# Attention and expert kernel: key and query parts stored in DRAM as 128-row blocks, read back in eight transfers a batch, with the query reads ahead of a row of maxima

## The reference

```python
q = proj(x1t, Wq, bq)                       # x1 = layernorm(x), 512 positions, 8 heads x 16
k = proj(x2t, Wk, bk)                       # x2 = ctx
v = proj(x2t, Wv, bv)
scores = jnp.einsum('bhqd,bhkd->bhqk', q, k) / jnp.sqrt(D_HEAD)
attn = jax.nn.softmax(scores, axis=-1)
out = jnp.einsum('bhqk,bhkd->bhqd', attn, v)
...
x = x + jnp.tanh(g_xattn[0]) * out
h = _rmsnorm(_layernorm(x), rms_weight)     # 4096 rows of 512
w_dense = top-2 of softmax(h @ router_w), normalised
moe = sum over e of w_dense[e] * (silu(h @ w_gate[e]) * (h @ w_up[e])) @ w_down[e]
sh = silu(h @ sw_gate) * (h @ sw_up) @ sw_down
x = x + jnp.tanh(g_ffn[0]) * (moe + sh)
```

## Time and profile before

| | |
|---|---|
| time, median of 3 runs | 1412.91 us (1408.93 to 1428.1) |
| the profiled execution, its own time | 1411.02 us |
| its span in the trace | 1409.1 us |
| PE, DVE, ACT, POOL busy | 92%, 69%, 62%, 61% of the span |
| attention, up to the last turning of maxima | 880 us |
| mean share of time in which the 16 DMA engines are busy | 72% from 376 to 867 us |

### The profile page before, as it was taken

The page is one execution under the profiler, slowest core; times in us unless marked ns, Lnnn a source line. Parts: engine busy times, 40 slices in busy tenths (PEclk is TensorE's granted clock), DMA queues, the critical chain, the costliest instruction groups (busy, mean ns, idle before and its releaser), DMA issues.

```text
span 1409.1 us, 34589 instructions
## 1 busy us (share of the span) xinstructions
PE 1290.6 (92%) x12274; PEld 680.4 (48%) x12274; DVE 974.3 (69%) x1661; ACT 874.1 (62%) x1720; POOL 863.3 (61%) x1267
## 2 busy tenths in 40 slices
PE   2899899999998899889999988799999999999997
PEld 0233333333333333323333332387788878888885
DVE  4988889999987798888889887556654323333332
ACT  2488788888877788778878876534334333333332
POOL 8547677767787687867787752640214555555553
PEclk7799999999999999999999999999999999999999
DMA  6567777777777677677777664376654888886565
GB/s 177 166 175 212 205 215 210 206 211 193 194 207 191 187 194 197 189 187 208 192 196 193 196 164 112 122 209 145 126 176 90 203 197 202 198 190 112 111 108 80
DMA packets 161348, 248.28 MB, mean 176 GB/s; under 512 B 33733, under 2 KB 58956, under 8 KB 161182
## 3 DMA queue, kind: packets, MB, share of 16 engines
q1 hardware_dynamic: 142926, 208.70, 53.5%
q0 software_dynamic: 18256, 37.38, 14.5%
HBM read 141.06 MB, written 103.88 MB: 174 GB/s over the span
## 4 chain that ended last, share of the span: by engine, by line
PE 42%; DMA 13%; SPq 12%; issue 12%; POOL 9%; DVE 9%; ACT 2%; POOLq 1%; DVEq 0%; another core or an unknown queue 0%; ACTq 0%
PE m_banks L969 19%; SPq L471 7%; PE bank L926 6%; PE bank L895 6%; DVE row_max L1142 6%; PE m_banks L873 4%; DMA arena<-pv_d 4%; DMA arena<-parts_q 4%; DMA parts_k<-arena 3%; PE bank L901 2%; POOL xs L793 2%; SPq L532 2%; PE bank L857 1%; PE bank L851 1%; PE bank L991 1%
## 5 line engine op out<-in xcount | busy, mean ns | idle before, releaser
L1142 DVE TENSOR_REDUCE row_max<-m_banks 128x2 f32<-128x1024 f32 x512 | 614.8, 1221 | 98.5 <-PE m_banks L873 89.7
L1426 ACT ACTIVATE arena<-bank 128x512 f32<-128x512 f32 x1024 | 554.4, 605 | 97.7 <-PE bank L895 89.9
L895 PE MATMUL bank<-arena 112*32 112x512 bf16 x4096 | 338.2, 384 | 11.9 <-ACT arena L1426 7.2
L926 PE MATMUL bank<-arena 128*32 128x512 f32 x2048 | 283.2, 603 | 1.9 <-issue 1.6
L895 PEld LDWEIGHTS bank<-arena 112*32 112x32 bf16 x4096 | 113.1, 95 | 275.5 <-ACT arena L1426 136.3
L873 PE MATMUL m_banks<-arena 48*128 48x512 bf16 x1024 | 176.6, 391 | 58.2 <-DMA arena<-parts_q 29.2
L805 POOL DMA_INDIRECT out<-xs,ids x71 | 112.3, 1581 | 172.9 <-ACT xs L1508 140.7
L969 PE MATMUL m_banks<-w_ring,h_hi 128*128 x568 | 183.0, 403 | 0.0
L1497 ACT ACTIVATE arena<-m_banks 128x256 f32<-128x256 f32 x103 | 39.5, 384 | 189.7 <-PE m_banks L969 179.3
L873 PEld LDWEIGHTS m_banks<-arena 48*128 48x128 bf16 x1024 | 40.3, 94 | 194.7 <-issue 83.2
L694 POOL TENSOR_TENSOR arena<-arena 128x512 f32<-128x512 f32 x32 | 40.9, 1279 | 122.8 <-DMA arena<-pv_d 119.4
(11 more groups left out here) (182 smaller groups left out, 1997.9 us busy)
## 6 DMA issues: line engine op xcount, KB each, us to landing
pv_d<-arena SPq DMA_DIRECT2D x32, 512.0 KB, 4.4
w_ring<-split_d SPq DMA_DIRECT2D x60, 256.0 KB
parts_k<-arena SPq DMA_DIRECT2D x96, 128.0 KB
parts_q<-arena SPq DMA_DIRECT2D x96, 128.0 KB
arena<-parts_k SPq DMA_DIRECT2D x64, 192.0 KB
arena<-parts_q SPq DMA_DIRECT2D x64, 192.0 KB
arena<-in_w SPq DMA_DIRECT2D x36, 256.0 KB, 7.2
arena<-in_ctx SPq DMA_DIRECT2D x32, 256.0 KB, 3.7
```

The source lines that it names most:

```text
L895: last = nc.tensor.matmul(out[c, :], k_stack[b % 3][0:SHIFTED, h, kt * P + c.start:kt * P + c.stop], q_stack[b % 3][0:SHIFTED, h, :], star ...
L926: last = nc.tensor.matmul(pv_ps[2 * DH * j:2 * DH * (j + 1), :], v_ones[b % 3][:, kt, GROUP * g + j, :], probs[pair % 3][:, j, :], start=( ...
L1142: nc.vector.reduce_max(pair, m_ps[(STEPS * b + u) // 2 % M_PAIRS], AX_X).then_inc(s_mx, 1)
L1426: nc.scalar.activation(probs[group % 3][:, j, :], bank_of["scores", b, s], ACT.Exp, scale=float(DH) ** -0.5).then_inc(s_exp, 1)
```

## The change

`parts_d` gets four parts in place of three: for keys low, middle, high, high, for queries high, high, middle, low, so that each of the two stacked orders is three parts that lie side by side. The rows of the key and query weights and biases are permuted on the host (`rows_first`), so that a projected row is (channel, head), as it is in DRAM. A batch's parts are then written by two transfers each for keys and queries: the high part twice in one transfer, the middle and low part in another, which waits for both. The middle and low part lie side by side in SBUF (`held`). The reads are 4 and 4 transfers where they were 6 and 6. In SP's list the middle and low part of the query goes ahead of the key reads, and the query reads go ahead of the reciprocals and of the row of maxima, which also change places. The two stores of an expert's row become one.

```diff
-STORED = ((LO, MID, HI), (HI, MID, LO))
-FIRST = ((MID, HI, HI), (HI, HI, MID))
-SECOND = ((LO, MID, HI), (HI, MID, LO))
...
+STORED = ((LO, MID, HI, HI), (HI, HI, MID, LO))
+HELD = ((HI, LO, MID), (HI, MID, LO))
+FIRST_AT, SECOND_AT = (1, 0), (0, 1)
+READS = 8
+WRITES = 2
...
-                    sp.wait_ge(s_part, 4 * b + 2 * n + part)
-                sp.dma_start(parts_d[n][b % 2][STORED[n].index(part)].rearrange("d h l -> h d l"), parts[n][part]
+                    sp.wait_ge(s_part, 4 * b + 2 * n + 2)
+                rows = parts_d[n][b % 2].rearrange("t d h l -> (d h) t l")
+                at = STORED[n].index(part if part == HI else HELD[n][1])
+                sp.dma_start(rows[:, at:at + 2, :],
+                             parts[n][HI].unsqueeze(1).broadcast_to([P, 2, L]) if part == HI else held[n][:, 1:3, :]
                              ).then_inc(s_wr[n], DMA)
...
-                    for row, parts_at in ((LANE * a, FIRST), (LANE * (1 - a), SECOND)):
-                        for at, part, k in stored_runs(parts_at, n):
-                            sp.dma_start(lane(stack[row + at * DH:row + (at + k) * DH, :, :], a),
-                                         lane(src[part:part + k].rearrange("t d h l -> (t d) h l"), a)
-                                         ).then_inc(s_rd[b % 3], DMA)
+                    for row, at in ((LANE * a, FIRST_AT[n]), (LANE * (1 - a), SECOND_AT[n])):
+                        sp.dma_start(lane(stack[row:row + STACK, :, :], a),
+                                     lane(src[at:at + 3].rearrange("t d h l -> (t d) h l"), a)
+                                     ).then_inc(s_rd[b % 3], DMA)
...
                 if is_b(i + 2):
-                    if i + 2 > 0:
-                        read(i + 2, 0)
                     write(i + 2, 1, MID)
-                    write(i + 2, 1, LO)
...
+                    read(i + 2, 0)
...
+                if is_b(i + 2):
+                    read(i + 2, 1)
+                if is_b(i - 1):
+                    store_reciprocals(i - 1)
                 if is_b(i + 1):
                     row(i + 1, 0)
-                if is_b(i - 1):
-                    store_reciprocals(i - 1)
-                if is_b(i + 2):
-                    read(i + 2, 1)
```

More of the change, by code:

```diff
@@ L151, in build @@
             under("below_staged", [P, B * EXPERTS + L], F32)
-            staged = [under(f"staged_{part}", [P, L]) for part in ("hi", "lo")]
+            staged_both = under("staged", [P, 2, L])
+        staged = [staged_both[:, part, :] for part in range(2)]
         arena = sb("arena", [P, ARENA])
@@ L162, in build @@
         rest = a.take(L)
-        parts = [[a.take(L // 2, BF16) for _ in range(3)] for _ in range(2)]
+        held = [a.take(3 * L // 2, BF16).rearrange("p (t l) -> p t l", t=3) for _ in range(2)]
+        parts = [[held[n][:, HELD[n].index(part), :] for part in (HI, MID, LO)] for n in range(2)]
         wq, wk, wv = (a.take(P) for _ in range(3))
@@ L268, in build @@
         bank_of = {}
-        parts_d = [[dram(f"parts_{n}{i}", (3, DH, HEADS, L), BF16) for i in range(2)] for n in "kq"]
+        parts_d = [[dram(f"parts_{n}{i}", (4, DH, HEADS, L), BF16) for i in range(2)] for n in "kq"]
         pv_d = dram("pv_d", (HEADS, 2 * DH, L), F32)
@@ L518, in store_staged @@
                 e, r = STAGED[k]
-                for part, done in enumerate((s_sh, s_sl)):
-                    sp.wait_ge(done, k + 1)
-                    sp.dma_start(split_d[e - IN_PLACE, part, :, r, :], staged[part][:].bitcast(F32)).then_inc(s_sst, DMA)
+                sp.wait_ge(s_sh, k + 1)
+                sp.wait_ge(s_sl, k + 1)
+                sp.dma_start(split_d[e - IN_PLACE].rearrange("t p r l -> p t r l")[:, :, r, :], staged_both[:].bitcast(F32)
+                             ).then_inc(s_sst, DMA)
             def source(j):
@@ L572, in _ @@
                 if is_b(i + 3):
-                    for part in (HI, MID, LO):
+                    for part in (HI, MID):
                         write(i + 3, 0, part)
@@ L576, in _ @@
                     if r == 2:
-                        sp.wait_ge(s_sst, 2 * DMA * len(STAGED))
+                        sp.wait_ge(s_sst, DMA * len(STAGED))
                     if r == 0:
@@ L680, in split @@
                 pool.wait_ge(s_part, 4 * b + 2 * n)
-                pool.wait_ge(s_wr[n], 3 * DMA * b)
+                pool.wait_ge(s_wr[n], WRITES * DMA * b)
                 hi, mid, lo = parts[n]
@@ L732, in staged_low @@
                 if k:
-                    pool.wait_ge(s_sst, 2 * DMA * k)
+                    pool.wait_ge(s_sst, DMA * k)
                 r = STAGED[k][1]
@@ L736, in staged_low @@
                     link(nc.gpsimd.tensor_scalar(staged_raw, staged_raw, w_rms[:, r:r + 1], None, ALU.mult))
[L737 removed]
+                nc.gpsimd.tensor_tensor(staged[LOW], staged_raw, staged[HI].bitcast(F32), ALU.subtract
                                         ).then_inc(s_sl, 1)
@@ L1407, in evacuate @@
                         act_e.wait_ge(s_part, 4 * (b - 1) + 2 * n + 2)
-                        act_e.wait_ge(s_wr[n], 3 * DMA * b)
+                        act_e.wait_ge(s_wr[n], WRITES * DMA * b)
                     nc.scalar.activation(proj[n], bank_of["projection", b, n], ACT.Identity, bias=bias[:, n:n + 1]).then_inc(s_evac, 1)
@@ L1446, in staged_high @@
                     act_e.wait_ge(s_sl, k)
-                    act_e.wait_ge(s_sst, 2 * DMA * k)
+                    act_e.wait_ge(s_sst, DMA * k)
                 r = STAGED[k][1]
                 if r < CHUNKS:
-                    nc.scalar.mul(staged[HI][:], staged_raw, w_rms[:, r:r + 1]).then_inc(s_sh, 1)
+                    nc.scalar.mul(staged[HI], staged_raw, w_rms[:, r:r + 1]).then_inc(s_sh, 1)
                 else:
-                    nc.scalar.copy(staged[HI][:], staged_raw).then_inc(s_sh, 1)
+                    nc.scalar.copy(staged[HI], staged_raw).then_inc(s_sh, 1)
             def exponentials(c):
@@ L1555, in ffn, with rows_first @@
         return inputs["L0_ffn_" + name]
+    def rows_first(v):
+        return v.reshape(HEADS, DH, -1).transpose(1, 0, 2).reshape(v.shape)
     gate = np.concatenate([ffn("sw_gate")[None], ffn("w_gate")])
```

7 lines of the change are left out of this document (3 added, 4 removed).

## The result

The changed kernel takes 1479.32 us (median of 4 runs, 1474.47 to 1488.35), the kernel before 1418.76 us beside it (4 runs, 1408.93 to 1428.1): a ratio of 1.0435, 95% interval 1.0338 to 1.0532. The forecast was 1390 us, a gain of 1.6%; it is a loss of 4.4%.

The account below looks back on a forecast made before the run. Attention's loop through SP and POOL, 27.3 us a turn, was taken as the bound. Savings of 16.4 us over 18 turns, 3 before them and 1 at the start, 20.4 from 1411.0, gave 1390 us; range for 8 in 10, 1369 to 1405.

Parts of the forecast that it names:

- the short loop: Attention, values' load through POOL's query split, query write and reads to the next load: 21.4 to 24.5 us a turn.
- Query reads, reciprocals, row of maxima: Step on SP's new order in attention: long loop 22.8 us a turn, short loop 21.4 to 24.5, both below 26.4.
- the values' landing: Term in attention's loops: values land 4.4 us after their load is issued, the trace's median, where 7.92 was measured.
- the short loop binds: Rival, chance 0.08: SP's wait for the query writes delays row and values' load; loop 28.0 us a turn, 1433 us.
- Its threshold: The short loop binds once the landings of values and queries together exceed 14.8 us; 8.8 to 12 was assumed.
- The loop over two turns: Attention before the change: values, POOL's list, keys, SP's issues, next values take 54.6 us, 27.3 a turn, and bind.
- The turns without a wait: Turns of PE with no wait for query parts, mean 26.4 us, PE and DVE full: the turn expected after the change.
- The extra 256 KB as no bound: Writes of a batch rise from 768 to 1024 KB; DMA share rises from 0.72 to 0.75, no new bound.
- The row of maxima behind the query reads as free: In SP's list the row can slip behind the query reads by several us before PE feels it.
- The query write ahead of the key reads: In SP's list its issue is hidden in the wait for key writes; cost nothing, at most 1 us of SP's time.
- POOL's wait for the values and the clock: Signs in attention: POOL's wait falls from 95 us to below 30; the granted clock rises from 0.99 to 1.00.
- a turn now starts with a wait: Sign of a wrong prediction: a turn of PE starts with a wait for a row of maxima or for the values.

Follow-up runs that it names:

- layout alone: The kernel before with the new DRAM parts, eight reads and one store of staged weights, SP's list in the old order: 1381.13 us, ratio 0.987.
- the five best kernels: Five follow-up kernels with the new parts and eight reads, differing in the order of SP's list or in ACT storing the reciprocals: ratios 0.978 to 0.987 to the kernel before.
- key reads, reciprocals, query reads, row: The change with key reads ahead of the query's middle and low part, and reciprocals ahead of the query reads, row of maxima behind: 1374.46 us, ratio 0.978.
- the reciprocals alone ahead: The change with only the store of reciprocals put back ahead of the query reads, row of maxima still behind them: 1381.12 us, ratio 0.984.

## Why the prediction was wrong

**The step that failed** is the sum of the short loop in *Query reads, reciprocals, row of maxima*: "values land 4.4, `add_attention` 3.6, split 3.55, write 0.4, its landing (4.4 to 7.55), reads 2.5, reciprocals, row and load 2.5". The loop was found, and found to be the one that a new order makes. But the load of the values waits for the reciprocals to have landed (`s_r`), and that landing has no term in it. It was left out without a reason. The old trace shows it almost nowhere, one wait of 2.0 us: six query reads stood between store and load and covered it for 3.8 us, and the new order takes this cover away. It measured 5.25 us in the round shown, and 5.1 to 9.1 with a median of 6.6 in the 27 rounds in which it is on the chain.

**The second term** mis-sized is the values' landing. I took 4.4 from the earlier trace rows as the median of the loads, on the ground that query reads no longer stand right ahead. Both were wrong. The 4.4 is of another transfer: of the two on `pv_d` the view gives a landing only for the store, `pv_d<-arena`, 512 KB. The loads' own semaphore, as far as its updates are recorded, puts them at 6.8 us at the median before the change and at 6.9 after it, and at 7.1 in the kernel that issues them ahead of the query reads. So the 7.92 and 6.79 of the earlier trace rows were near the ordinary, and query reads ahead weren't what made them. The issues of the kernel before, with KB each and the median us to landing where it is known:

```profile
pv_d<-arena SPq DMA_DIRECT2D x32, 512.0 KB, 4.4
...
arena<-pv_d SPq DMA_DIRECT2D x32, 256.0 KB
```

In the new order the query reads are still just ahead of the load: only reciprocals and row lie between, 16 and 8 KB. The load measured 8.78 in the round shown. With 5.25, 8.78, 7.1 for POOL, 7.1 from the query write to the end of the query reads, and 0.8 of issues, the loop is 29.1. The rest of my sum was near: I had 4.4 at least for the write's landing, in whose place stand 4.1 of key reads and three small issues.

**The rival that came true** is *the short loop binds*, with a chance of 0.08. Its place was right and its price, 1433, too low by 46 us: its loop of 28.0 lacked the reciprocals' landing, and only the 7.55 that it put for the query write, against 4.1, made up part of it. What I held against it was the 4.4 of the wrong transfer. Its threshold, two landings above 14.8, was wrong as well: here they were 12.9 with the issues that replaced one, and the third landing closed the gap. The threshold should have counted every landing on the loop, not the two that the old trace names.

**What was right.** The loop over two turns as the bound of the kernel before fits: with layout alone, which takes issues out of it, the waits fall and the time is 1381. It isn't shown, since layout alone changes the writes as well. The turns without a wait as the end of the gain: the five best kernels are at 0.978 to 0.987 of the one before, beside 0.985 in the forecast, and in the two of them called layout alone and key reads, reciprocals, query reads, row, the turns in the stretch of the earlier trace rows take 26.2 and 26.1 us at the mean, beside the 26.4 that I took. That they reach the forecast is no merit of the sum, which was made for an order that doesn't: in each of the five the reciprocals' store goes ahead of the query reads or is issued by ACT. The extra 256 KB as no bound: layout alone moves 186 GB/s over the span, and it is faster. The row of maxima behind the query reads as free: shown by the kernel with the reciprocals alone ahead. *The query write ahead of the key reads* was put at 0 to 1 us of slack; with the old order behind it, it costs 0.8%, which the intervals don't confirm. But it is what sets the eight reads close together, and with them half of the reciprocals' price: taken out of the change alone, the ratio falls from 1.044 to 1.006.

**Of the signs** that I named, SP's issues fell from six to four reads as said, and the wait for query parts went. From the first key read to the load of the reciprocals it was to take 9 us in place of 14, and it took 13.3 (403.80 to 417.06): what the issues saved, the wait for the landing took back. POOL's wait for the values and the clock went the other way, and "a turn now starts with a wait" was the right alarm, though the wait for a row of maxima came in the middle of the turn, at the row of the second half.

## What to carry to other kernels

When a list of transfers is put in a new order, ask of each instruction that waits for a landing what used to be issued between the store and that wait: that was its cover, and the old trace shows hardly a wait for it. A small transfer on a critical loop is to be issued ahead of the large ones, by another engine if its own comes too late; another queue alone didn't help where the large ones were already issued. A move that looks free because it only fills a wait can take away the pause in which the queue drained. And before a landing time goes into a sum, check which of two transfers on one tensor it belongs to.

## What the runs showed of the hardware

A store of 16 KB took longer to land when reads had been issued just before it, by either engine. Between the end of its issue and its last landing on the semaphore it took, at the median, 1.1 us in layout alone, with a row of 8 KB just ahead; 3.9 with the query reads just ahead and the key reads before a pause; 4.8 in the kernel with the reciprocals alone ahead, behind the key reads, context, tokens and x; 5.9 behind all of these and the query reads (in layout alone the load that waits for it still goes out only after 2.6 us, since SP is busy with the query reads). From ACT's queue it took 6.5 to 7.8 us behind the first of the query reads. Yet the DMA engines were busy only 70% of attention in the change. A mean share says nothing of the line in front of one transfer. The expert half is 7 us shorter in the change than before, with no line of it changed; no run was made to find out why.
